# Loads of x, attention results and denominators in 128 KB parts, spread over the pairs of scores

## The reference

```python
x = x + 0.5 * ffn(layernorm(x))          # [x, -x] @ k0, relu*2, @ k1, relu*2, @ k2; k = +1 or -1
x = x + attention(layernorm(x))          # 16 heads of 16, 2048 keys, softmax, then @ wo.T + bo
x = x + 0.5 * ffn(layernorm(x))          # the same weights again
```

## Time and profile before

| | |
|---|---|
| three runs | 1490.06, 1490.13, 1495.2 us; median 1490.13 |
| the profiled execution's own time | 1485.83 us |
| its span, first to last instruction | 1481.8 us, so 4.03 us lie around it |
| granted TensorE clock | 1.000 over the whole span |
| busy: PE, ACT, DVE, POOL | 1467.2, 1149.8, 594.7, 59.8 us |
| transfers | 103.93 MB, 70 GB/s on average |
| attention | from about 270 to 1403 us |

### The profile page before, as it was taken

The page is one execution under the profiler, slowest core; times in us unless marked ns, Lnnn a source line. Parts: engine busy times, 40 slices in busy tenths (PEclk is TensorE's granted clock), DMA queues, the critical chain, the costliest instruction groups (busy, mean ns, idle before and its releaser), DMA issues.

```text
span 1481.8 us, 69894 instructions
## 1 busy us (share of the span) xinstructions
PE 1467.2 (99%) x32431; PEld 754.9 (51%) x32431; DVE 594.7 (40%) x1330; ACT 1149.8 (78%) x1240; POOL 59.8 (4%) x65
## 2 busy tenths in 40 slices
PE   9999999999999999999999999999999999999999
PEld 4555455544455445545454554564555455445454
DVE  7546755621432253334332332332242342333461
ACT  3221221799999999999999999999899999999821
POOL 2010111001000100010100000000000000000000
PEclk9999999999999999999999999999999999999999
DMA  4121324313221341223222221322212312313010
GB/s 137 49 86 36 92 72 107 95 43 96 74 58 43 102 100 47 72 87 101 90 53 74 81 60 58 89 59 61 84 47 69 86 43 71 87 49 64 25 43 17
DMA packets 113359, 103.93 MB, mean 70 GB/s; under 512 B 58919, under 2 KB 98599, under 8 KB 113063
## 3 DMA queue, kind: packets, MB, share of 16 engines
q1 hardware_dynamic: 112230, 98.61, 25.1%
q10 hardware_dynamic: 832, 0.79, 0.2%
HBM read 61.87 MB, written 25.43 MB: 59 GB/s over the span
## 4 chain that ended last, share of the span: by engine, by line
PE 98%; DVE 1%; DMA 1%; issue 0%; SPq 0%; ACT 0%
PE psum L875 31%; PE psum L916 31%; PE psum L896 14%; PE psum L769 12%; PE psum L781 3%; PE psum L757 3%; PE psum L788 2%; PE psum L801 1%; DMA den_t<-den_rows 0%; DVE den_t L1135 0%; DMA x_sb<-in_x 0%; PE psum L794 0%; DVE stats L1059 0%; DVE xn L1001 0%; SPq L1273 0%
## 5 line engine op out<-in xcount | busy, mean ns | idle before, releaser
L971 ACT ACTIVATE prob<-psum 128x1024 f32<-128x1024 f32 x1024 | 1032.0, 1026 | 64.1 <-PE psum L896 25.6
L916 PE MATMUL psum<-prob,v_sb 64*17 64x512 f32 x8192 | 552.7, 589 | 0.2 <-issue 0.2
L896 PE MATMUL psum<-q_st,k_st 64*32 64x512 f16 (+1 forms) x7736 | 481.3, 376 | 3.2 <-issue 3.1
L944 ACT ACTIVATE h_hi<-psum 128x512 f16<-128x512 f32 x183 | 108.3, 597 | 211.4 <-PE psum L769 165.8
L896 PEld LDWEIGHTS psum<-q_st,k_st 64*32 64x32 f16 (+1 forms) x7736 | 154.1, 92 | 203.2 <-ACT prob L971 77.5
L916 PEld LDWEIGHTS psum<-prob,v_sb 64*17 64x17 f32 x8192 | 152.7, 93 | 147.4 <-issue 80.0
L1011 DVE SCALAR_TENSOR_TENSOR h_lo<-psum,h_hi 128x512 f16<-128x512 f32 x256 | 168.3, 687 | 82.8 <-ACT h_hi L944 80.3
L1009 DVE TENSOR_SCALAR h_hi<-psum 128x512 f16<-128x512 f32 x73 | 50.5, 692 | 369.4 <-PE psum L875 369.4
L875 PE MATMUL psum<-h_lo,w 64*32 64x512 f16 (+1 forms) x4688 | 165.0, 376 | 2.0 <-issue 1.9
L875 PE MATMUL psum<-h_hi,w 64*32 64x512 f16 (+1 forms) x4688 | 164.6, 376 | 0.3 <-ACT h_hi L944 0.2
L875 PEld LDWEIGHTS psum<-h_hi,w 64*32 64x32 f16 (+1 forms) x4688 | 84.7, 93 | 60.6 <-issue 11.0
(11 more groups left out here) (110 smaller groups left out, 878.6 us busy)
## 6 DMA issues: line engine op xcount, KB each, us to landing
k_st<-k_halves SPq DMA_DIRECT2D x256, 128.0 KB, 2.8
q_halves<-piece SPq DMA_DIRECT2D x32, 256.0 KB, 2.5
q_st<-q_halves SPq DMA_DIRECT2D x64, 128.0 KB, 2.6
x_rows<-x_sb SPq DMA_DIRECT2D x16, 256.0 KB, 2.2
k_halves<-piece SPq DMA_DIRECT2D x16, 256.0 KB, 3.0
att_rows<-o_sb SPq DMA_DIRECT2D x128, 32.0 KB
x_sb<-x_rows SPq DMA_DIRECT2D x8, 512.0 KB, 4.5
att_t<-att_rows SPq DMA_DIRECT2D x16, 256.0 KB
```

The lines of the kernel that those rows point to most:

```text
L896: mm = pe.matmul(psum[c, SCORES[(h + r) % len(SCORES)], :], k_st[rows, slot, t * P:(t + 1) * P][:, c], q_st[rows, slot, :], start=True, st ...
L916: mm = pe.matmul(psum[32 * j:32 * j + va, O_BANKS[r], :], v_sb[rows, b * key_tiles + t, GROUP * g4 + j, :], prob[rows, h % PROBS, :], star ...
L944: act.activation(hi, psum[:, bank, :], ACT.Relu).then_inc(act_done, 1)
L971: act.activation(prob[:, to:to + 2, :], psum[:, bank:bank + 2, :], ACT.Exp, scale=score_scale / QK_SCALE ** 2).then_inc(exp_sem, 1)
```

## The change

A load of x that is met during attention is now four transfers of 128 KB (one tile of 128 tokens each), and each fetch is four of 128 KB: results of 64 partitions, their denominators, and the same for the other 64. They stand in a list `moves`, parts of fetches ahead of parts of loads. One is taken at each pair of scores that `MOVE_TURNS` names (1, 3, 6, 8, 11, 13, 16, 18, 21, 23, 25, 27, 29, 31 of a group's 32) and waits on `qk_sem` for that pair. What is left at the end of attention is issued without such a wait. "Heads" are laid only when the parts they read have been laid. The waits for free buffers stand ahead of the first part. Loads and fetches on the path behind the flag keep their size or get four parts without waits.

```diff
@@ -240,17 +241,34 @@ def lay_idle(n):
             s = side.pop(0)
             if s.kind == "fetch":
                 held.append(s)
+            elif s.kind == "load":
+                loaded_in_parts.append(s.u)
+                moves.extend(Step("load", s.u, part) for part in range(tpb))
...
         while held and n > group_steps * (block_groups * (held[0].u - blocks) + 2 * (held[0].m + 1)):
-            lay(held.pop(0), SHARED, False)
+            lay_fetch()
+
+    def lay_fetch():
+
+        s = held.pop(0)
+        lay(s, SHARED, False)
+        before = sum(f.kind == "part" for f in moves)
+        moves[before:before] = [Step("part", s.u, s.m, lo=part) for part in range(2 * FETCH_PARTS)]
+
+    def lay_move(after):
+
+        s = moves.pop(0)
+        s.after = after
+        work.append(s)
 
     def lay_long(most):
 
         def unfetched(s):
-            return s.kind == "heads" and any((f.u, f.m) <= (s.u, s.m // tpb) for f in held)
+            return s.kind == "heads" and any(
+                f.kind != "load" and (f.u, f.m) <= (s.u, s.m // tpb) for f in held + moves)
@@ -279,6 +297,8 @@
     KEY_TURNS = [5 * k // 2 for k in range(2 * (KEY_PARTS + 1))]
+    MOVE_TURNS = [turn + 1 for turn in KEY_TURNS] + [25, 27, 29, 31]
+    FETCH_PARTS = 2
@@ -288,6 +308,8 @@ def lay_score(no, narrow=False):
         if no % GROUP_SCORES in KEY_TURNS and no // GROUP_SCORES + 1 < groups:
             work.append(Step("keys", no // GROUP_SCORES + 1, KEY_TURNS.index(no % GROUP_SCORES)))
+        elif no % GROUP_SCORES in MOVE_TURNS and moves:
+            lay_move(no)
         work.append(Step("score", n, pair, narrow=narrow))
@@ -356,7 +378,9 @@
     while held:
-        lay(held.pop(0), SHARED, False)
+        lay_fetch()
+    while moves:
+        lay_move(0)
@@ -1131,7 +1160,7 @@ def dve_heads(s):
-            dve.wait_ge(att_in[half], 16 * 2 * (no + 1))
+            dve.wait_ge(att_in[half], 16 * 2 * FETCH_PARTS * (no + 1))
@@ -1198,16 +1227,31 @@ def sp_steps(steps):
-                elif s.kind == "load":
-                    sp_load(u)
+                elif s.kind == "load" and u in loaded_in_parts:
+                    if m == 0:
+                        sp_free_x(u)
+                    if s.after:
+                        sp.wait_ge(qk_sem, s.after)
+                    load_x_part(u, m)
...
+                elif s.kind == "part":
+                    if s.lo == 0:
+                        sp_fetch(u, m)
+                    if s.after:
+                        sp.wait_ge(qk_sem, s.after)
+                    sp_fetch_part(u, m, s.lo)
@@ -1286,11 +1329,17 @@ def sp_fetch(u, half):
-            sp.dma_start(att_t[:, half, :], att_dram[half * P:(half + 1) * P, cols]).then_inc(att_in[half], 16)
-            sp.dma_start(den_t[:, half, :], den_dram[half * hs:(half + 1) * hs, cols].unsqueeze(1).broadcast_to(
-                (hs, hd, BANK))).then_inc(att_in[half], 16)
+            rows = slice(part // 2 * hs * hd, (part // 2 + 1) * hs * hd)
+            row = half * P + part // 2 * hs * hd
+            if part % 2 == 0:
+                sp.dma_start(att_t[rows, half, :], att_dram[row:row + hs * hd, cols]).then_inc(att_in[half], 16)
+            else:
+                sp.dma_start(den_t[rows, half, :], den_dram[row // hd:row // hd + hs, cols].unsqueeze(1).broadcast_to(
+                    (hs, hd, BANK))).then_inc(att_in[half], 16)
```

More of the change, by code:

```diff
@@ L46 @@
     free_o: int = 0
+    after: int = 0
     narrow: bool = False
@@ L234, in build @@
     LONG = {"norm": 1.0, "xn": 0.3, "split": 0.4, "flip": 1.0, "merge": 0.4, "heads": 0.26, "peak": 0.3}
-    waiting, held = [], []
+    waiting, held, moves, loaded_in_parts = [], [], [], []
     def lay_idle(n):
@@ L576, in x_loads @@
         def x_loads(u):
-            return u // RING + 1 - (u % RING == 0)
+            return sum(tpb if v in loaded_in_parts else 1 for v in range(u % RING, u + 1, RING) if v)
         def load_x(u):
@@ L583, in load_x, with load_x_part @@
             sp.dma_start(x_sb[:, u % RING], (x_tiles if u < blocks else x1_tiles)[:, ts, :]).then_inc(x_in[u % RING], 16)
+        def load_x_part(u, t):
+            i = block_of(u)
+            sp.dma_start(x_sb[:, u % RING, t, :], (x_tiles if u < blocks else x1_tiles)[:, i * tpb + t, :]
+                         ).then_inc(x_in[u % RING], 16)
         def load_x0(queue, t):
@@ L1200, in sp_steps @@
                         sp_keys(0, part)
-                elif s.kind == "load":
-                    sp_load(u)
+                elif s.kind == "load" and u in loaded_in_parts:
[4 more added lines that the diff above has]
+                    load_x_part(u, m)
+                elif s.kind == "load":
+                    sp_free_x(u)
+                    load_x(u)
+                elif s.kind == "part":
[4 more added lines that the diff above has]
+                    sp_fetch_part(u, m, s.lo)
                 elif s.kind == "flip":
@@ L1208, in sp_steps @@
                                  transpose=True).then_inc(flipped, 16)
-                elif s.kind == "fetch":
+                elif s.kind == "fetch" and u >= redo:
                     sp_fetch(u, m)
+                    for part in range(2 * FETCH_PARTS):
+                        sp_fetch_part(u, m, part)
                 elif s.kind not in FILLS or not s.last():
@@ L1230, in sp_steps, with sp_free_x @@
                                  x_sb[:, u % RING, m * per_bank:(m + 1) * per_bank, :]).then_inc(x_out[u % RING], 16)
-        def sp_load(u):
+        def sp_free_x(u):
             old = u - RING
@@ L1288, in sp_fetch, with sp_fetch_part @@
                 sp.wait_ge(mm_done, before.mm)
+        def sp_fetch_part(u, half, part):
+            i, hs = block_of(u), P // hd // FETCH_PARTS
             cols = slice(i * BANK, (i + 1) * BANK)
-            hs = P // hd
-            sp.dma_start(att_t[:, half, :], att_dram[half * P:(half + 1) * P, cols]).then_inc(att_in[half], 16)
-            sp.dma_start(den_t[:, half, :], den_dram[half * hs:(half + 1) * hs, cols].unsqueeze(1).broadcast_to(
-                (hs, hd, BANK))).then_inc(att_in[half], 16)
+            rows = slice(part // 2 * hs * hd, (part // 2 + 1) * hs * hd)
[5 more added lines that the diff above has]
+                    (hs, hd, BANK))).then_inc(att_in[half], 16)
         g_words = prob[:].rearrange("p s c -> p (s c)")
```

1 line of the change is left out of this document (removed).

## The result

| | before | after |
|---|---|---|
| median of the runs (range, count), us | 1490.1 (1489.7 to 1495.2, 6) | 1481.2 (1480.0 to 1482.9, 6) |
| the profiled execution, us | 1485.83 | 1479.96 |
| its span, us | 1481.8 | 1476.1 |

The ratio is 0.9934, with an interval of 0.9915 to 0.9954: 8.9 us less by the medians, where 4.3 us were forecast. Both profiled executions were quicker than the medians of their kernels, that of before by 4.3 us and that of after by 1.2.

The account below looks back on a forecast made before the run. PE was taken as the bound, with 5.44 us idle in attention waiting for instructions. Gain 4.7 less 0.4 added gave -4.3 us from 1490.13, so 1485.8 us; range 1480.8 to 1490.0, the forecast alone 1484.4 to 1488.7.

Parts of the forecast that it names:

- The mechanism: In attention, PE's instruction packets on q8 come late behind 1.5 MB of transfers SP issues together; up to 5.44 us idle.
- No change: Rival, 1490.1 us: parts only move the lateness, q8 packets being late for a reason of their own; chance 0.16.
- The gain: PE's pauses in attention: 4.7 us of the 5.44 us idle go, from 2.9 to 5.4.
- a constant offset of the two ways of timing: Explanation of the 4.3 us between the profiled execution of before and the runs' median, kept unchanged after the change.
- a larger gain: Rival, 1481.5 us: the 4.3 us between profiled execution and runs are also such pauses and go too; chance 0.18.
- The rest of 0.7 us beside transposing transfers: Pauses expected to remain at two blocks, near 536 and 680 us, where a transposing transfer stands between parts; 0 to 2.5 us.
- the 1.5 us that I named: Sign of being right: all PE pauses with "issue" before them between 281 and 1399 us together stay under 1.5 us.
- Waits that are added: Inside attention, later reciprocals, x loads, transposing transfers and extra SP issues were all to cost 0.
- A DVE wait on den_t above 8 us: Sign of being wrong: such a wait of DVE for the denominators inside attention.
- the margin that I had called nil: Near attention's end, h_hi and h_lo done at 1403.1 against the attention result's copy at 1403.17; cost 0 to +0.5, taken 0.1.
- 80 more issues: Extra transfers issued by SP, 0.3 to 0.6 us each, paid out of SP's idle time; cost 0.
- The end of attention: Last fetch in four issues instead of two, nothing covering it: +0.3 us, from -0.3 to +1.0; with reciprocals +0.4.

Follow-up runs that it names:

- e1: Changed kernel's 128 KB parts, but all of a fetch or load issued together where the whole transfers stood; 1493.7 us, ratio to before 1.0019.
- e2: Changed kernel with whole transfers of 512 and 256 KB, each waiting for its own pair of scores; 1481.9 us, ratio to before 0.9947.
- e3: Changed kernel with only the very last fetch, behind the end of attention, again two whole 256 KB transfers; 1479.1 us, ratio to before 0.9931.
- e4: Half of the change: loads of x in spread parts, the four transfers of a fetch whole and issued together; 1487.3 us, ratio to before 0.9992.
- e5: The other half of the change: fetches in spread parts, each load of x whole in one issue; 1483.5 us, ratio to before 0.9966.
- e6: Changed kernel plus eleven bursts of unused 256 KB stores, 0.5 to 3 MB each, on all 16 DMA engines; one run, 1481.4 us.
- before_c: The kernel before, unedited, profiled a third time; one run, 1492.1 us, with 9.74 us of PE idle in attention.
- after_again: The changed kernel, unedited, timed and profiled once more; 1481.7 us, ratio to before 0.9948.
- e10: Changed kernel with fetches halved by columns (all 128 partitions, half of the 512 tokens) instead of by partitions; 1479.4 us, ratio to before 0.9921.
- before_b: The kernel before, unedited, profiled a second time; one run, 1484.5 us, with 4.47 us of PE idle in attention.
- e12: Changed kernel with fetches halved by columns, last fetch whole, no part taken while a transposing transfer is due; 1479.0 us, ratio to before 0.9941.
- e11: Changed kernel plus the same eleven store bursts as e6, shaped to run on eight DMA engines; one run, 1488.6 us.
- e15: e12 with each row of denominators stored twice in DRAM, so den_t is read from 16 rows; 1481.5 us, ratio to before 0.9944.

## Why the prediction was right or wrong

**The mechanism: right.** PE stood without instructions behind the transfers that SP issued together, and spacing them removes it. The times of q8's packets tie the pauses to them. The 16 profiles hold 40 pauses of PE over 0.3 us between 281 and 1396 us, and every one ends 1.2 to 1.6 us after a packet of q8 has ended. For the earlier trace rows that packet ended at 541.09, 675.88 and 1042.48, and PE went on at 542.52, 677.35 and 1043.98. At 676 and 1042 us it started late, 6.8 and 7.2 us after the one before; at 541 it took 3.09 us, the longest in attention, where the median is 1.05. e1 and e2 separate this from the size of a transfer (which is worth something of its own, e2 against e3), e4 and e5 name the fetch as the part that counts most. "No change" falls with after itself. The rule in the Trainium skill ("DMA: Bandwidth & Descriptors", Queues, rings and completion order) that each engine takes its queues in turn is then no reason for no gain: stores on all engines leave q8 time enough in e6, real fetches do not.

**The gain: mis-sized, the step that failed.** The working took the pauses of one profiled execution, 5.44 us, as the pauses of the kernel, and gave the 4.3 us between that execution and the median to "a constant offset of the two ways of timing". There is no such offset: the profiled executions of before_c, after_again and e10 are slower than the medians beside them, by 1.3, 0.7 and 2.1 us. before_b and before_c, profiled once each, took 1484.5 and 1492.1 us with idle sums of 4.47 and 9.74. That is 7.6 us of time for 5.27 us of shown idle, or 1.44 for one, falls of the clock included. By that slope, drawn through two executions, the median of 1490.1 has about 8.4 us of shown idle (an estimate), and taking it down to 0.87 gives 10.8 us; with the 2.09 us lost at the end this is 8.7, and 8.9 were measured. The rival "a larger gain" (1481.5) had this mechanism and its price, and I gave it 0.18. What I should have weighed more is the 5 us between runs of before: the runs beside the experiments spread from 1483.4 to 1499.4 us (69 runs), those of kernels with spread fetches by 1.6 to 3.5 us.

From the forecast of -4.3 to the measured -8.9 it goes as follows. In the profiled executions PE came to the end of attention 7.7 us earlier and not 4.7: 3.0 us more. The end cost 2.1 and not 0.4: 1.7 less. The median of before lies 4.3 us above its profiled execution and that of after only 1.2, where I had the same distance for both: 3.1 more. That makes -8.7, and 0.2 us lie around these marks.

Two things let before lose more than its idle time shows. The granted clock falls behind some of the longest pauses (before_c above; none fell in attention in the profiles of the earlier trace rows and of before_b). And PE loses time that is not shown as idle: set side by side by the starts of their exps, the profiled executions of before and after draw apart by 1.46 us where 1.10 of idle is shown, by 2.43 where 1.86 is the earlier trace rows, by 0.56 near 938 us, behind a fetch, where none is, and by 7.4 over attention, where the idle sums differ by 5.44 - 0.87 = 4.57. A likely reason is that the ends of matmuls are modelled and overlap, but no run tests it. So even between the profiled executions attention gained 7.4 us and not 4.7.

**The rest of 0.7 us beside transposing transfers: right.** 0.84 us at 682.30, and e12 shows the cause. All pauses together are under the 1.5 us that I named, one is over the 0.5. The packets of q8 were to come every 4 to 5 us; near 676 us they do but for one distance of 5.7.

**Waits that are added: right, with one sign misread.** The first reciprocal of the block at 688.35 us now starts at 685.48, 2.87 us earlier, and by the exps PE is 2.87 us ahead there: it is where it was. A DVE wait on den_t above 8 us did come inside attention, 11.36 us to 1389.87, which I had named as a sign of trouble. It costs nothing: DVE had nothing else to do before it, and the copy of the attention result, the margin that I had called nil, starts at 1395.45, 7.72 us earlier than in the earlier trace rows, as much as PE is ahead. The step's 0.1 us was 0. The "80 more issues" are 32 + 24 = 56 (64 transfers for 32, 32 loads for 8), which changes nothing, since they cost nothing.

**The end of attention: mis-sized.** I took +0.3 from a range of -0.3 to +1.0; it was 6.27 - 4.09 = 2.18 us between the last store and the denominators, and 2.09 us for PE, beyond the 1.5 that I had named as a sign of being wrong. The fourth transfer leaves at 1402.18, 1.72 us behind the store, where I had 1.4. What failed is the price of the transfer, 2.7 us: 64 partitions of repeated rows take 4.55 us for 128 KB, more than the 3.65 us of the whole 256 KB. My upper bound had assumed that half the bytes cannot take longer. e3 gives 4.57 us from store to landing with one whole transfer, e10 5.18 with eight rows. The DMA shares in 40 slices show why: of before from 1408.3 to 1412.5 us, then of after from 1400.5 to 1407 us.

```profile
DMA  0000000004699576889866564465465120000000
```
```profile
DMA  1000000056435634437742222121223221100000
```

The last third of after's fetch moves at 0.1 to 0.3 of the engines, where before had 0.4 to 0.6. The Trainium skill ("DMA: Bandwidth & Descriptors", Why a DMA increments its semaphore by 16 and not by 1) says that a transfer runs on the largest number of engines up to 16 that divides the slowest dimension of both sides: eight for eight rows, four for four. The trace agrees with half and a quarter of the engines. The same page's warning (Rules for kernel authors) against splitting into halves by partitions, which the prediction quoted and then bounded too low, holds at this place, though not for the reason it gives, that both halves use all 16 engines: here the half runs on fewer.

**The total.** -8.9 us against -4.3: what pauses cost a typical execution about 11 (the estimate above) in place of 4.7, the end +2.1 in place of +0.4. The time lies within the range given only because the range was widened for the rival; it is outside the 1484.4 to 1488.7 of the forecast alone.

**What stays open.** Why q8's packet is late behind a fetch. Stores of up to 3 MB on all engines do not do it, stores at half of the engines' time do at three of four places where PE takes packets fast, reads into SBUF of 1 MB at once do, with den_t over eight or sixteen rows. Direction, the share of the engines, the keys queued behind and whether a packet happens to be due are all possible. Nor is it known what makes the pauses of one execution twice as long as those of another.

## What to carry to other kernels

When an engine that is the bound pauses on "issue" behind transfers that are issued together, spread them over the work; the spacing counts most (e1 against after_again is 12 us), the size of each less (e2 against e3 is 2.8 us). Size such a gain from several profiles, or from the spread of the runs: here the runs of before differed by 16 us, its three profiles had 4.5, 5.4 and 9.7 us of pauses, and the quickest showed the least. Keep whole the transfer that nothing covers, and cut by the dimension that leaves the number of rows as it was.

## What was new about the hardware

- A fetch can stop PE's supply of instructions at 0.69 of the DMA engines' time and 212 GB/s, and stores at 0.91 and 328 GB/s do not. PE goes on 1.2 to 1.6 us after the packet of q8 has ended, in 40 pauses of 40, and before's pauses at 676 and 1042 us came when 6.8 and 7.2 us lay between two packets.
- Pauses of PE of 2.45 and 2.36 us were followed by 3.4 us at 1.2 GHz, those of 2.16 and 2.69 in the same execution were not, and neither was the wait of 3.58 us in after's profile. At the end of attention, behind waits of 1.9 to 4.0 us, it happened in 12 of the 16 profiles, for 3.4 us in nine and 6.8 in three (after_again, e11, e15), not in after and the three of before. So the longer end of after may cost some executions more than its 2.09 us. Here is e12, from the wait to the products behind it, with 8 matmuls in 3.4 us; after did 14 in the 3.6 us from 1409.4, its pause of 0.41 included:

```profile
1406.60:1409.00 2.40, 0.07 (x1) 0.10 (x1) 2.33 (x5) 0.60 (x1) 0.00 (x0) 1.00 0.00 0
1409.00:1412.40 3.40, 3.40 (x8) 2.72 (x9) 3.33 (x7) 0.00 (x0) 0.00 (x0) 0.50 0.00 0
```
- A read of four rows into 64 partitions took 4.55 to 4.93 us for 128 KB (six profiles), of eight rows into 128 partitions 3.59 (e10), and 256 KB from eight rows 3.65 to 4.44 (seven profiles).
